# A gated cross-attention block with a routed feed-forward: a new order of loads and of feed-forward steps in the output stage, and the 128 sums of the output weights on VectorE

## The reference, cut to what matters

```
h   = layernorm(x)                                       # 8 x 128 x 512
q   = rmsnorm(h) @ w_q.T ; k = ctx @ w_k.T ; v = ctx @ w_v.T      # 32 heads
s   = softmax(q k^T + bias, masked)
x1  = x + tanh(g_xattn) * (h + (s v) @ w_out.T)          # w_out: 512 x 4096
n   = layernorm(x1)
p   = softmax(n @ W_router.T) ; the 2 best of 8 experts, renormalised
y   = n @ W_base.T + b_base + sum of the 2 experts' low-rank parts (rank 16)
out = x1 + tanh(g_ffn) * y
```

## Time and profile before

| | us |
|---|---|
| median of three runs | 878.59 |
| the profiled execution's own time | 878.36 |
| its span, first to last instruction | 876.6 |
| PE busy | 837.9 |
| DVE busy | 627.1 |
| ACT busy | 494.6 |
| POOL busy | 294.6 |

### The profile page before, as it was taken

One profiled execution on the slowest core, in us unless ns is written; L12 is line 12 of the kernel. 1 busy time (PEld: TensorE's weight loads), 2 busy tenths in 40 slices (PEclk: granted clock), 3 DMA queues, 4 the chain that ended last, 5 costly groups with the idle time before them and its releaser, 6 DMA issues.

```text
span 876.6 us, 13049 instructions
## 1 busy us (share of the span) xinstructions
PE 837.9 (96%) x4318; PEld 708.8 (81%) x4318; DVE 627.1 (72%) x981; ACT 494.6 (56%) x1153; POOL 294.6 (34%) x310
## 2 busy tenths in 40 slices
PE   8899999999999999999999999999977799997888
PEld 7688887888888888888888888888865588875676
DVE  5776476577688888888788878887743687766345
ACT  4546655456666666666666666666643965542110
POOL 1213230013455563736536545555250000040120
PEclk9999999999999999999999999999998899998699
DMA  8365456595565466645556467557768988851001
GB/s 315 125 180 175 126 176 197 168 283 179 180 211 178 150 196 199 210 144 176 192 177 210 143 183 226 175 161 236 269 224 329 388 298 289 278 211 37 25 0 73
DMA packets 131298, 168.52 MB, mean 192 GB/s; under 512 B 9248, under 2 KB 83872, under 8 KB 130592
## 3 DMA queue, kind: packets, MB, share of 16 engines
q1 hardware_dynamic: 131232, 167.70, 59.2%
HBM read 111.04 MB, written 62.91 MB: 198 GB/s over the span
## 4 chain that ended last, share of the span: by engine, by line
PE 75%; DMA 7%; DVE 7%; ACT 3%; POOL 3%; issue 2%; SPq 2%; DVEq 0%; ACTq 0%; POOLq 0%
PE bank L324 60%; PE bank L1454 6%; PE bank L1471 5%; DMA t_raw<-t_spill 4%; PE bank L1462 3%; DVE t_hl L985 1%; DMA s_piece<-in_w_o 1%; ACT t_hl L861 1%; DMA t_spill<-g_at 1%; DMA raw_v<-in_w_v 1%; DVE stats L989 1%; DVE s_hl L985 1%; DVE wv L985 1%; DMA t_spill<-x_at 1%; DVE acc L1216 1%
## 5 line engine op out<-in xcount | busy, mean ns | idle before, releaser
L324 PE MATMUL bank<-t_hl,s_hl 128*128 128x512 f32 x672 | 172.9, 419 | 15.6 <-DVE s_hl L985 15.6
L324 PE MATMUL bank<-xb,wq 128*128 128x512 f32 x672 | 177.3, 399 | 0.0
L324 PE MATMUL bank<-cb,wq 128*128 128x512 f32 x672 | 177.2, 399 | 0.0
L324 PEld LDWEIGHTS bank<-t_hl,s_hl 128*128 128x128 f32 x672 | 135.6, 205 | 47.1 <-DVE s_hl L985 14.9
L324 PE MATMUL bank<-wv,cb 128*128 128x512 f32 x672 | 156.5, 394 | 4.2 <-DVE wv L985 3.8
L324 PEld LDWEIGHTS bank<-wv,cb 128*128 128x128 f32 x672 | 126.6, 189 | 32.9 <-DVE wv L985 5.9
L645 POOL TENSOR_TENSOR bm<-bias_sb,mneg 128x512 f32<-128x512 f32 x64 | 75.1, 1174 | 200.8 <-DVE pr L1146 165.0
L324 PEld LDWEIGHTS bank<-cb,wq 128*128 128x128 f32 x672 | 121.8, 188 | 23.0
L324 PEld LDWEIGHTS bank<-xb,wq 128*128 128x128 f32 x672 | 121.7, 188 | 22.9
L985 DVE TENSOR_TENSOR t_hl<-t_raw,t_hl 128x1024 fp32r<-128x1024 f32 x56 | 68.6, 1225 | 68.6 <-ACT t_hl L861 68.6
L861 ACT ACTIVATE t_hl<-t_raw 128x1024 fp32r<-128x1024 f32 x56 | 59.2, 1057 | 86.0 <-PE bank L324 54.2
(11 more groups left out here) (157 smaller groups left out, 1230.5 us busy)
## 6 DMA issues: line engine op xcount, KB each, us to landing
t_raw<-t_spill SPq DMA_DIRECT2D x56, 512.0 KB, 4.4
v_spill<-stage SPq DMA_DIRECT2D x64, 256.0 KB, 2.9
raw<-in_w_qk SPq DMA_DIRECT2D x32, 512.0 KB, 5.5
v_sb<-v_spill SPq DMA_DIRECT2D x64, 256.0 KB, 3.1
s_raw<-s_spill SPq DMA_DIRECT2D x56, 256.0 KB, 4.6
t_spill<-x_at SPq DMA_DIRECT2D x48, 256.0 KB, 3.3
s_piece<-in_w_o SPq DMA_DIRECT2D x64, 128.0 KB, 3.5
s_spill<-s_piece SPq DMA_DIRECT2D x32, 256.0 KB, 3.6
```

Source lines behind the costliest of these rows:

```text
L324: mm = pe.matmul(dst, a, b, start=first and n == 0, stop=last and n == total - 1, skip_group_check=True)
```

## The change

- Value stage: token sum 3 of the context moves from GpSimd to VectorE, ahead of weight sum 3; GpSimd keeps sums 2 and 4, and sum 4 now also waits for the low weight part of M7.
- Attention stage: `s_sums` moves from GpSimd to VectorE, in even steps, behind `probabilities(s + 1)` and ahead of the early splits. `t_sum` stays on GpSimd.
- Loads: `EARLY_LOADS` hold 14 units, each up to one step earlier; ScalarE and VectorE split unit 10 behind the last attention step instead of in it. Load 14 is the first thing in SP's list behind the attention steps, then `store_sums(64)`, load 15, `store_sums(65)`, load 16, `store_sums(66)`. The wait for all stores moves to behind load 18.
- The feed-forward's inputs: x comes as eight loads of 256 KB behind units 18 to 24 and 28 to 34, b_base behind 26, w_lora 36, w_base as four quarters 38 to 44, w_up 46. What is done with each (`ffn_hi`, `ffn_lo`) stands two units later on ScalarE and VectorE.
- The feed-forward's steps are taken batch by batch and in a new order, on TensorE, ScalarE and VectorE.

```diff
 EARLY_SPLITS  ... (PAIRS - 1, 2): (7, 8), (PAIRS - 1, 3):
-                (9, 10)}
+                (9,)}
-EARLY_LOADS = {(PAIRS - 2, 0): (0, 1), (PAIRS - 2, 1): (2, 3), (PAIRS - 2, 2): (4,), (PAIRS - 2, 3): (5,), (PAIRS - 1, 0): (6, 7),
-               (PAIRS - 1, 1): (8,), (PAIRS - 1, 2): (9, 10), (PAIRS - 1, 3): (11, 12)}
+EARLY_LOADS = {(PAIRS - 2, 0): (0, 1), (PAIRS - 2, 1): (2, 3, 4), (PAIRS - 2, 2): (5,), (PAIRS - 2, 3): (6,), (PAIRS - 1, 0): (7, 8),
+               (PAIRS - 1, 1): (9, 10), (PAIRS - 1, 2): (11, 12), (PAIRS - 1, 3): (13,)}
-FIRST_SPLIT = 11
-FIRST_LOAD = 13
+FIRST_SPLIT = 10
+FIRST_LOAD = 14
+X2_AT = (18, 20, 22, 24, 28, 30, 32, 34)
+BB_AT = 26 ; LORA_AT = 36 ; BASE_AT = (38, 40, 42, 44) ; UP_AT = 46
 # SP
             for n in range(FIRST_LOAD, UNITS):
                 load_o(n)
+                if n < FIRST_LOAD + 3:
+                    store_sums(STEPS + n - FIRST_LOAD)
+                if n == X2_AT[0]:
+                    ... the waits for all stores
+                if n in X2_AT:
+                    t = X2_AT.index(n)
+                    sp.dma_start(acc[:, t, :], x[:, ORDER[t], :]).then_inc(x2_in[t], 16)
 ...
 # GpSimd, context tokens
-            pool.wait_ge(wv_lo_ok, 3)
+            pool.wait_ge(wv_lo_ok, VORD.index(M5) + 1)
             token_sum(2, ctx_q, ct_ok, cb_lo_ok)
-            token_sum(3, ctx_q, ct_ok, cb_lo_ok)
             pool.wait_ge(ctx_in[1, 0], 16)
+            pool.wait_ge(ct_ok, 3)
+            pool.wait_ge(wv_lo_ok, VORD.index(M7) + 1)
             token_sum(4, ctx_q, ct_ok, cb_lo_ok)
 # GpSimd, attention steps
                 t_sums(s)
-                if s % 2 == 0:
-                    s_sums(s // 2)
 # VectorE
                 if g == 0 and i in (2, 3):
+                    if i == 2:
+                        ve.wait_ge(ctx_in[1, 1], 16)
+                        ve.wait_ge(ct_ok, 2)
+                        ve.wait_ge(cb_lo_ok, VORD.index(M5) + 1)
+                        ve.tensor_tensor(tt[0], ctx_q(1, 1), ctx_q(0, 1), ALU.subtract).then_inc(ct_ok, 1)
                     wv_sum(0, i + 1)
 ...
+            def s_sums(r):
+                a11, a21, a12, a22 = s_piece[:, 0, 0, :], s_piece[:, 0, 1, :], s_piece[:, 1, 0, :], s_piece[:, 1, 1, :]
+                ve.wait_ge(piece_in, 32 * r + 32)
+                ve.tensor_tensor(a22, a21, a22, ALU.add).then_inc(piece_ok, 1)
+                ve.tensor_tensor(a21, a11, a21, ALU.subtract).then_inc(piece_ok, 1)
+                ve.wait_ge(piece_ok, 4 * r + 2)
+                ve.tensor_tensor(a11, a22, a11, ALU.subtract).then_inc(piece_ok, 1)
+                ve.wait_ge(piece_ok, 4 * r + 3)
+                ve.tensor_tensor(a12, a12, a11, ALU.subtract).then_inc(piece_ok, 1)
 ...
                     if s + 1 < STEPS:
                         probabilities(s + 1)
+                    if s % 2 == 0:
+                        s_sums(s // 2)
                     for n in EARLY_SPLITS.get((p, j), ()):
                         o_lo(n)
 # VectorE, from unit 45 on
+            add_output(0) add_output(1) o_lo(45) o_lo(46) ffn_lo(46) add_output(2) o_lo(47) o_lo(48) ffn_lo(48)
+            center(0) o_lo(49) center(1) o_lo(50) o_sum(5) o_lo(51) add_output(3) o_lo(52) center(2) o_lo(53)
+            center(3) o_lo(54) tokens1_lo(0) tokens1_lo(1) o_lo(55) tokens1_lo(2) tokens1_lo(3) routing(0)
+            hwt_lo(0) routing(1) add_output(4) add_output(5) finish(0) finish(1) center(4) center(5) hwt_lo(1)
+            add_output(6) tokens1_lo(4) tokens1_lo(5) add_output(7) center(6) center(7) routing(2) finish(2)
+            tokens1_lo(6) tokens1_lo(7) finish(3) hwt_lo(2) routing(3) finish(4) finish(5) hwt_lo(3) finish(6) finish(7)
 # TensorE (the calls of a line stand under each other in the code; o = output)
-            o(8..41) out_transposes(0) out_transposes(1) o(42..44) x1_transposes(0) x1_transposes(1) o(45) lora(0)
-            o(46..48) hw_transposes(0) out_transposes(2) out_transposes(3) o(49) base(0) o(50) base(1) up(0)
-            x1_transposes(2) x1_transposes(3) o(51) lora(1) o(52..55) hw_transposes(1) base(2)
-            out_transposes(4) out_transposes(5) base(3) up(1) out_transposes(6) out_transposes(7)
-            x1_transposes(4) x1_transposes(5) lora(2) x1_transposes(6) x1_transposes(7) base(4) base(5) ...
+            o(8..40) out_transposes(0) out_transposes(1) out_transposes(2) o(41..46) x1_transposes(0) o(47)
+            x1_transposes(1) o(48) out_transposes(3) o(49) o(50) x1_transposes(2) o(51) x1_transposes(3) o(52)
+            lora(0) o(53) o(54) hw_transposes(0) o(55) lora(1) out_transposes(4) out_transposes(5) base(0) base(1)
+            hw_transposes(1) up(0) base(2) x1_transposes(4) out_transposes(6) x1_transposes(5) out_transposes(7)
+            base(3) lora(2) base(4) up(1) x1_transposes(6) x1_transposes(7) base(5) hw_transposes(2) lora(3)
+            base(6) up(2) base(7, (0, 1)) hw_transposes(3) base(7, (2, 3))
```

More of the change, by code:

```diff
@@ L973, in _ @@
+            tokens1_hi(0)
+            o_hi(51)
+            tokens1_hi(1)
+            o_hi(52)
+            o_hi(53)
+            o_hi(54)
+            tokens1_hi(2)
+            o_hi(55)
+            tokens1_hi(3)
+            router_exp(0)
+            hwt_hi(0)
+            o_copy(NP - 1)
+            router_exp(1)
             hwt_hi(1)
-            o_copy(NP - 1)
-            tokens1_hi(2)
+            tokens1_hi(4)
+            tokens1_hi(5)
             router_exp(2)
-            tokens1_hi(3)
+            tokens1_hi(6)
@@ L978, in _ @@
+            tokens1_hi(7)
             hwt_hi(2)
@@ L1313, in _ @@
[L1313 to L1325 removed]
+            add_output(0)
+            add_output(1)
+            o_lo(45)
@@ new lines, in _ @@
+            o_lo(46)
+            ffn_lo(46)
+            add_output(2)
+            o_lo(47)
+            o_lo(48)
+            ffn_lo(48)
+            center(0)
+            o_lo(49)
+            center(1)
+            o_lo(50)
+            o_sum(5)
+            o_lo(51)
+            add_output(3)
+            o_lo(52)
+            center(2)
+            o_lo(53)
+            center(3)
+            o_lo(54)
+            tokens1_lo(0)
+            tokens1_lo(1)
+            o_lo(55)
+            tokens1_lo(2)
@@ L1326, in _ @@
+            tokens1_lo(3)
+            routing(0)
+            hwt_lo(0)
             routing(1)
-            hwt_lo(1)
             add_output(4)
             add_output(5)
-            center(2)
+            finish(0)
+            finish(1)
+            center(4)
+            center(5)
+            hwt_lo(1)
             add_output(6)
-            tokens1_lo(2)
+            tokens1_lo(4)
+            tokens1_lo(5)
             add_output(7)
-            center(3)
-            finish(1)
+            center(6)
@@ L1576, in up @@
                                  first=False).then_inc(y_ps, 1)
-            for n in range(DUOS, 5 * DUOS + 2):
+            for n in range(DUOS, 5 * DUOS + 1):
                 output(n)
@@ L1581, in _ @@
             out_transposes(1)
-            for n in range(42, 45):
+            out_transposes(2)
+            for n in range(41, 47):
                 output(n)
             x1_transposes(0)
+            output(47)
             x1_transposes(1)
-            output(45)
-            lora(0)
-            for n in range(46, 49):
-                output(n)
-            hw_transposes(0)
-            out_transposes(2)
+            output(48)
             out_transposes(3)
             output(49)
-            base(0)
             output(50)
-            base(1)
-            up(0)
             x1_transposes(2)
+            output(51)
             x1_transposes(3)
-            output(51)
+            output(52)
+            lora(0)
+            output(53)
+            output(54)
+            hw_transposes(0)
+            output(55)
             lora(1)
-            for n in range(52, 56):
-                output(n)
-            hw_transposes(1)
-            base(2)
             out_transposes(4)
             out_transposes(5)
+            base(0)
+            base(1)
+            hw_transposes(1)
+            up(0)
+            base(2)
+            x1_transposes(4)
+            out_transposes(6)
+            x1_transposes(5)
+            out_transposes(7)
             base(3)
+            lora(2)
+            base(4)
             up(1)
-            out_transposes(6)
-            out_transposes(7)
-            x1_transposes(4)
-            x1_transposes(5)
-            lora(2)
             x1_transposes(6)
             x1_transposes(7)
-            base(4)
             base(5)
```

206 lines of the change are left out of this document (89 added, 117 removed).

## The result

The changed kernel takes 832.1 us (median of four runs, 831.04 to 834.29) against 878.2 us for the kernel before (876.86 to 879.08): a ratio of 0.948, 95% interval 0.9454 to 0.9505. That is 46 us less. 838 were forecast, so the change gained 5.9 us more than the forecast said. The profiled execution took 832.98 us, its span is 831.0 us.

The account below looks back on a forecast made before the run. TensorE bounds the kernel, gapless at full clock in attention, with 55 us of waits and slow clock in three places elsewhere. Gains of 3.9 + 0 + 17.4 + 19.1 = 40.4 us from 878.4 give 838 us, range 826 to 854.

Parts of the forecast that it names:

- Value stage: Token sum 3 on VectorE removes TensorE's 2.24 us wait and the slow clock behind it: gain 3.9 us.
- 128 sums: Attention stage: weight sums on VectorE take 291 ns each, 1.2 us a call, under 2.3 us of cover: gain 0.
- the forecast's own sign: Attention stage: sums near 290 ns, up to 500, and still no TensorE wait from 200 to 568 us.
- walk through the last steps: Last six attention steps followed by durations: TensorE waits about 1.1, 0.6, 1.5 and 3.3 us ahead of unit 7.
- place 2: Change from attention to output, 636 to 690 us: 25 us lost to waits and slow clock, 17.4 to be gained.
- Loads: Attention to output: with the new load order unit 16 begins at 672 us, not 689.51; gain 17.4 us.
- rival D: Output units: loads late all the same, sharing DMA engines with extra loads and stores; 848 us, chance 0.1.
- Tail: From 760 us: new order wins 19.1 of 26.4 us, leaving 2 of waits and 5 of clock.
- The floor of 823 us: Whole kernel: what is left if all 55 us of TensorE waits and slow clock were won.
- A: Last steps and tail: cover holds, hardly a wait in the tail; 50 us gained, 828 us, chance 0.27.
- B: Output and tail: waits move, VectorE late for output units or GpSimd's bias additions delaying `rstd1`; 853 us, chance 0.22.
- C: Attention stage: VectorE becomes the pace, TensorE waits every second step; slower, 956 us or 898 at half, chance 0.03.

Follow-up runs that it names:

- experiment 2: Kernel before with only the new order of loads, early loads and splits, x as two loads behind unit 18: 863.4 us against 879.2.
- experiment 10: Changed kernel with 31 of 32 groups of weight sums on GpSimd, the last on VectorE, load of unit 11 ahead of the last piece store: 828.0 us.
- experiment 4: Changed kernel with all 128 weight sums back on GpSimd: 825.0 us; in a second run 824.6 us against 831.7 for the changed kernel.
- experiment 8: Changed kernel with only the last 4 of 32 groups of weight sums back on GpSimd: 826.2 us.
- experiment 9: Kernel before with the new tail order and late, dealt-out loads of x and weights; other loads and all sums as before: 842.3 us, 0.9598.
- experiment 6: Changed kernel with the narrow matmuls of the four router and adapter steps made twice: 843.4 us.
- experiment 7: Changed kernel with the first two router steps directly behind their tokens' last transposes, ahead of units 52 to 55: 842.2 us.
- experiment 1: Kernel before with only token sum 3 moved to VectorE: 875.8 us against 879.2.

## Why the forecast held, point by point

- **Value stage, 3.9 us; measured 4.7.** Token sum 3 runs on VectorE from 24.87 to 26.1, half a microsecond earlier than said. The wait and the slow clock of the earlier trace rows are both gone. The 1.7 us for the clock are right for the executions that show it; experiment 2 shows the same wait without it.
- **128 sums, 291 ns each; measured 284 to 292.** In the steady stage I took 0; one wait of 1.2 us for `pr` came (at 205 us, behind the first call, whose load made VectorE wait 3.29 us), 1.3 in all. By the forecast's own sign, no TensorE wait for `pr` there, this term was wrong, by that much. The lengthening by 1068/685 that the forecast allowed for, from GpSimd's additions, doesn't show, because the two never met: not one of the 128 sums overlaps a GpSimd instruction in the trace. The one that does, in experiment 10, took 1.38 us. What costs is what the forecast had only in its walk through the last steps: VectorE is in order and waits for the piece, 9.0 us in five calls, 4.0 of them in the two calls shown above. The walk gave TensorE waits of 1.1, 0.6, 1.5 and 3.3 us; the trace has 0.78, 0.91, 0.84, 0.19 and 3.15. But I never set these against the gain in place 2: that they are the price of one separable part, 7 us, only experiments 4 and 8 showed.
- **Loads, unit 16 at 672 us, place 2 worth 17.4; measured 670.8** (648.97 + 8 x 2.73) **and 17.0.** Load 13 is issued at 651.27, as the walk had it (651), 5.4 us behind load 12: the gap is shorter than the 8.9 us of before, not gone, and the ring of four now covers it. And 366 GB/s at full share carried the dealt-out loads, so rival D was not seen. The number holds because it was worked out from where unit 16 would start. The cause was half mistaken: I put the old delay on ScalarE's late copy and on SP's waits for the stores, but 9.3 us of it came with the inputs in the same burst, above all from x, its loads and ScalarE's 5.74 us of work on it (experiment 9).
- **Tail, 19.1 us; measured 25.3. This is the term that was mis-sized**: 6.2 us, more than the whole difference of 5.2 us between the traces (45.6 against 40.4; 5.9 by the medians). Of the 26.4 us to be won I left 7.3, "2 of waits and 5 of clock"; 0.2 us of waits and no slow clock remained. The waits that I found at `x1_transposes(0)` and `lora(2)` aren't in the trace. The clock I had tied to "the waits and `lora` (narrow matmuls)". Experiment 6 takes out the second as a cause by itself (twice the narrow matmuls, clock 1.00). In experiment 7 one wait is back and with it the slow clock (2.85 us of wait, clock 0.77), though there the narrow matmuls stand right behind the wait. So the 5 us of clock were kept back for nothing: without the 12.9 us of waits there was no slow clock left. (The forecast took the clock's loss over whole windows, the idle time in them included; that 25.3 of the 26.4 us were won gives no sign that this was too much.)
- **The floor of 823 us** that the first part of the forecast read off is nearly reached by experiment 4, 824.6 us.
- **The rivals.** A (828) is nearer to 832.1 than the forecast of 838, in part by luck: it had the tail nearly right, 23 against 25.3, but place 2 at 23 against 17.0, since the cover in the last steps that it counted on did not hold. B had VectorE late for the output units: TensorE waits 3.15 us for unit 7, but from 648.97 us on only 0.2 us in all. C had VectorE as the pace of the attention stage; it is 89% busy in the steady stage and TensorE waits once.

## What to carry to other kernels

A wait on TensorE in a dense stage costs its length and, in most of these traces but not in all, the slow clock behind it (after the same 2.24 us it was 0.57, 0.57, 0.72 and 1.00). The slow clock is no item of its own: once the waits of the tail are gone, count it as gone too. Before work is moved from an idle engine to a busy one, ask what it waits for and not only how long it runs: 1.2 us of sums are cheap, but 2 us of waiting for their load stand in front of everything on an in-order queue. When a large load comes in the middle of a dense stage, deal out the work on it as well as the load: ScalarE's 5.74 us in one piece held up TensorE as the transfer did. And where a change has several parts that all help one stretch, price each in the company of the others: alone, the moved sums cost nothing that could be measured, since a later wait covered them, and with that wait gone they cost 7 us.

## What was not expected of the hardware

- The 128x128 sum on VectorE takes 284 to 292 ns where no GpSimd instruction runs beside it, and 1.38 us in the one call that meets it. VectorE's wide splits beside an unbroken row of GpSimd's 128x512 sums take 2.3 us, not 1.22, and the narrow ones 1.8, not 0.68 (experiment 10). These GpSimd sums grow from 1.28 to 1.74 us, one to 2.28: VectorE has most of the loss. The Trainium skill, page "SBUF — State Buffer", section "Who interferes with whom", has a VectorE instruction with two SBUF inputs and a GpSimd instruction that reads SBUF contend for a shared port that one of them holds at a time; the trace agrees in that both are held up.
- 128x136 matmuls follow each other every 0.112 us at the full clock for 48 in a row (experiment 6), and the clock stays at 2.4 GHz; behind 2.85 us of idling the same matmuls fall to one in 0.213 us after the first 14 (experiment 7).
- The same wait of TensorE, 2.24 us at 33 us in the same code, was followed by a granted clock of 0.57, 0.57, 0.72 and 1.00 in four traces (experiment 1).
